# Output projection of an attention kernel: two batches in one 256-column matmul, in other places of TensorE's order

## The reference

```
# cross attention: q from layernorm(x), k and v from ctx, 16 heads of 8 features
score = einsum('bhij,bhkj->bhik', k, q) / sqrt(8)
attn  = softmax(score, axis=1)                 # over the heads
out   = einsum('bhik,bhij->bhjk', attn, v)
out   = out.transpose(0, 2, 1, 3).reshape(B, -1, 64).transpose(0, 2, 1)
x     = x + out @ Wo_w.T + Wo_b
# feed-forward on layernorm(x): three blocks of
#   y = gelu(layernorm(qlora_linear(h))); h = h + qlora_linear(y)
x     = x + ffn(layernorm(x))
```

## Time and profile before

| | us |
|---|---|
| median of 3 runs | 396.86 (396.68 to 397.3) |
| the profiled execution's own time | 397.27 |
| its span | 395.5 |
| TensorE busy (matmul) | 355.0 |
| VectorE busy | 345.6 |
| ScalarE busy | 289.6 |
| GpSimd busy | 283.1 |

### The profile page before, as it was taken

The page is one execution under the profiler, slowest core; times in us unless marked ns, Lnnn a source line. Parts: engine busy times, 40 slices in busy tenths (PEclk is TensorE's granted clock), DMA queues, the critical chain, the costliest instruction groups (busy, mean ns, idle before and its releaser), DMA issues.

```text
span 395.5 us, 12974 instructions
## 1 busy us (share of the span) xinstructions
PE 355.0 (90%) x4717; PEld 250.7 (63%) x4717; DVE 345.6 (87%) x863; ACT 289.6 (73%) x542; POOL 283.1 (72%) x349
## 2 busy tenths in 40 slices
PE   2788899999999999999897867789999999999964
PEld 1344566677766676677565645577778877887631
DVE  4618999999999999999999999688999999888852
ACT  3458888888878898788765443557888888888741
POOL 5463998888988898888998787757776667734320
PEclk9999999999999999999999989999999999999995
DMA  5755766558655775458424000000000100110111
GB/s 159 177 172 188 222 189 186 171 180 239 186 162 158 210 217 181 140 177 240 152 88 139 3 0 2 2 1 2 28 28 27 53 27 27 29 53 29 38 44 53
DMA packets 53123, 43.29 MB, mean 109 GB/s; under 512 B 4497, under 2 KB 46945, under 8 KB 53089
## 3 DMA queue, kind: packets, MB, share of 16 engines
q1 hardware_dynamic: 53088, 42.84, 36.0%
HBM read 26.05 MB, written 16.78 MB: 108 GB/s over the span
## 4 chain that ended last, share of the span: by engine, by line
PE 58%; DVE 20%; POOL 8%; issue 7%; ACT 4%; DMA 1%; DVEq 0%; POOLq 0%; ACTq 0%
PE score_ps L983 8%; DVE zsum L554 6%; PE att_ps L948 6%; DVE negmax L533 6%; PE score_ps L888 5%; PE wo_ps L840 5%; PE work L1030 4%; POOL probs L377 3%; PE score_ps L877 3%; PE work L904 3%; PE att_ps L1030 3%; PE score_ps L1030 3%; PE score_ps L976 2%; PE score_ps L834 2%; PE work L908 2%
## 5 line engine op out<-in xcount | busy, mean ns | idle before, releaser
L377 POOL TENSOR_TENSOR probs<-probs,rz 128x1024 f32<-128x1024 f32 x64 | 136.0, 2142 | 27.2 <-DVE rz L557 26.8
L413 POOL TENSOR_TENSOR rs<-ve,minus_half 128x8 f32<-128x8 f32 (+1 forms) x40 | 55.6, 1390 | 53.4 <-DVE ve L520 53.4
L533 DVE TENSOR_REDUCE negmax<-score_ps 128x64 bf16<-128x1024 f32 x64 | 75.3, 1177 | 6.9 <-PE score_ps L877 6.7
L663 ACT ACTIVATE probs<-score_ps 128x1024 f32<-128x1024 f32 x64 | 65.7, 1026 | 18.5 <-PE score_ps L888 18.2
L554 DVE TENSOR_REDUCE zsum<-probs 128x64 f32<-128x1024 f32 x64 | 77.3, 1209 | 1.3 <-ACT probs L663 1.3
L755 ACT ACTIVATE z<-score_ps,nmr,rs 128x128 f32<-128x128 f32 x160 | 60.4, 469 | 15.3 <-POOL nmr L416 15.2
L888 PE MATMUL score_ps<-negmax,ident_bf 128*128 128x512 bf16 x128 | 39.2, 388 | 8.3 <-DVE negmax L533 8.2
L840 PEld LDWEIGHTS wo_ps<-wo_t,att_t 128*128 128x128 f32 x256 | 37.5, 193 | 13.8 <-issue 12.2
L948 PE MATMUL att_ps<-probs,v_diag 128*32 128x64 f32 x2048 | 43.9, 225 | 2.1 <-POOL probs L377 1.9
L983 PEld LDWEIGHTS score_ps<-lin_t,h 128*128 128x128 f32 x320 | 42.1, 192 | 1.3
L983 PE MATMUL score_ps<-lin_t,h 128*128 128x128 f32 x320 | 42.2, 275 | 0.0
(11 more groups left out here) (152 smaller groups left out, 719.9 us busy)
## 6 DMA issues: line engine op xcount, KB each, us to landing
q_parts<-parts SPq DMA_DIRECT2D x16, 512.0 KB, 3.6
q_stack<-q_parts SPq DMA_DIRECT2D x64, 128.0 KB, 3.0
k_stack<-k_parts SPq DMA_DIRECT2D x32, 256.0 KB, 3.3
ctx_sb<-in_ctx SPq DMA_DIRECT2D x16, 256.0 KB, 3.7
k_parts<-parts SPq DMA_DIRECT2D x16, 256.0 KB, 3.0
out<-x_all SPq DMA_DIRECT2D x16, 256.0 KB, 2.3
x_all<-in_x SPq DMA_DIRECT2D x14, 256.0 KB, 3.9
x_all<-in_x SPq DMA_DIRECT2D x1, 512.0 KB, 4.9
```

Of the source, the lines that this page charges most:

```text
L377: nc.gpsimd.tensor_tensor(e[:, :, :, :], e[:, :, :, :], by_query.broadcast_to([P, BANDS, SEQ, ADJ]), ALU.mult).then_inc(s_probs, 1)
L413: nc.gpsimd.tensor_tensor(rs2[b][:, lo:hi], ve2[b][:, lo:hi], minus_half[:, lo:hi], ALU.pow).then_inc(p_rs[b], 1)
L533: nc.vector.tensor_reduce(negmax[p % 2][:, :], score_ps[p % 2][:, :].rearrange("p (h k) -> p k h", k=SEQ), AX_X, ALU.max, negate=True).the ...
L663: nc.scalar.activation(probs[p][:, :, :, :], score_ps[p % 2][:, :].rearrange("p (u s k) -> p u k s", s=ADJ, k=SEQ), ACT.Exp, scale=SCALE). ...
```

## The change

`project_out` takes a token tile u instead of a part t, and one matmul covers both batch halves, 256 columns, with the same weights. A chunk has 4 such matmuls instead of 8. The bias rows and tile 0 stand in position 1, behind the q matmul, and tile 1 in position 2, behind the k matmul, both for chunk c-2. Positions 0 and 3 have no output projection any more. The waits for att_t and for the sum of the chunk before move with the bias rows.

```diff
--- before.py
+++ after.py
@@ -833,12 +833,11 @@
                 src = src.unsqueeze(1).broadcast_to([P, TPC, P])
                 nc.tensor.matmul(dst, pick_row[:, which, :], src, start=True, stop=False, skip_group_check=True)
 
-            def project_out(t, att):
-
-                b, u = t % 2, t // 2
+            def project_out(u, att):
+
                 for o in range(2):
-                    ins = nc.tensor.matmul(wo_ps[:, TILE * t:TILE * (t + 1)], att[:, o, TILE * u:TILE * (u + 1)],
-                                           wo_t[:, o, b, :], start=False, stop=o == 1, skip_group_check=True)
+                    ins = nc.tensor.matmul(wo_ps[:, 2 * TILE * u:2 * TILE * (u + 1)], att[:, o, TILE * u:TILE * (u + 1)],
+                                           wo_t[:, o, :, :], start=False, stop=o == 1, skip_group_check=True)
                 return ins
 
             def chunk(c, par, half):
@@ -919,16 +918,14 @@
                                                    start=False, stop=True, skip_group_check=True)
                         ins.then_inc(s_v_ps, 1)
 
-                    if p == 3 and live(c - 1):
-                        pe.wait_ge(s_att_t, c)
-                        if some(c - 1):
-                            pe.wait_ge(s_x2, c - 1)
+                    if p == 1 and live(c - 2):
+                        pe.wait_ge(s_att_t, c - 1)
+                        if some(c - 2):
+                            pe.wait_ge(s_x2, c - 2)
                         bias_rows(wo_ps[:, :], 1)
-                        project_out(0, att_t[1 - par])
-                    if p < 3 and live(c - 2):
-                        ins = project_out(p + 1, att_t[par])
-                        if p == 2:
-                            ins.then_inc(s_wo, 1)
+                        project_out(0, att_t[par])
+                    if p == 2 and live(c - 2):
+                        project_out(1, att_t[par]).then_inc(s_wo, 1)
 
                     mc, mp = (c, p - 2) if p >= 2 else (c - 1, p + 2)
                     if live(mc):
```

## The result

| | before, us | changed, us | ratio |
|---|---|---|---|
| first comparison | 396.77 (4 runs) | 406.36 (404.81 to 406.79, 4 runs) | 1.0235 (1.0204 to 1.0265) |
| the changed kernel again | 397.24 (11 runs) | 404.27 (403.35 to 406.21, 6 runs) | 1.0186 (1.0152 to 1.022) |

A forecast was written before the change was run, and what follows sets the result against it. TensorE and VectorE were read as near full, with ScalarE's order limiting what TensorE could save. Cycles 7.6, less 0.4, plus 0.3 gave +7.5 us on 397.27: 404.8 profiled, median 404.4, range 400.0 to 406.0.

The forecast's parts named there:

- The pass: TensorE's output projection: a 256-column fp32 pass taken as 0.213 us, a block of four as 0.85, the 0.10 gap kept.
- rival C: Half the penalty: gap hidden, -0.2 a cycle, vanished x_all waits give back 2 us; +3.3, 400.2 us; chance 0.12.
- rival B: Width nearly free in TensorE's projection: 0.11 us a pass, cycle 12.52, 395.1 us, or no change; chance 0.05.
- T to Q: From position 3's scores (T) to position 1's query projection (Q): falls from 7.13 to 6.79 us, limited by ScalarE's order.
- Rival A: VectorE, not ScalarE's order, is the bound: cycle can fall to 12.44, 2.6 us off, 394.3 us; chance 0.07.
- Q to T: From the query projection to the next position 3 scores: 5.58 us grows by 1.03, less 0.03; nothing hides it.
- The cycle: One attention chunk, position 3's scores to the next: 13.37 us against 12.68, +0.69, over 11 cycles 7.6.
- Rival D: As forecast, plus 0.2 us a cycle from GpSimd's chain or lost overlap: +9.7, 406.6 us; chance 0.06.
- Chunks 13 to 17: Late chunks: -0.4 us of lateness given back, +0.3 for chunk 13's own cost, wider blocks hidden from chunk 14 on.
- at nothing, +-0.5: TensorE's three bias-row waits for the sum into x_all, 3.9 us, mostly vanish without VectorE profiting: nothing, +-0.5 us.
- The median: Whole kernel: profiled execution 404.8 us taken as 0.4 above the median, so median 404.4.
- Other engines: In the longer cycle VectorE's waits grow without effect, GpSimd's chain counts at nothing, no DMA moves.

The follow-up runs named there:

- width_spread: Changed kernel with its 256-column matmuls back in the old places, one in each position; 397.1 us, ratio to before 1.0014.
- after_filled: Changed kernel with extra bias matmuls in TensorE's two longest negmax waits, 8 in chunk 13 and 14 in chunk 15; 404.52 us, ratio to before 1.0218.
- after_half_xln: Changed kernel with two of the four normalisations of x left out from chunk 3 on; 401.68 us, ratio to before 1.0123.
- width_only: Changed kernel with bias rows and tile 0 moved to position 3, tile 1 to position 0, still 256 columns; 405.41 us, ratio to before 1.0203.
- tiles_p0_p2: Changed kernel with bias rows and tile 0 moved to position 0, tile 1 in position 2, 256 columns; 402.96 us, ratio to before 1.0166.

## Why the prediction was right or wrong

- *The pass.* Taken as 0.213, measured 0.215; four take 0.96 with the gap, so 0.85 and 0.10 stand. The gap isn't hidden, which takes rival C out, and the end of the bounds at 0.11 (rival B) is out. width_spread shows what the width makes alone: nothing. The Trainium skill (TensorE: Matmul & The Clock Gate, Back-to-back issue gap) gives 81 ns for a bf16 matmul of 128 columns and 131 ns for one of 512, from which the prediction read that width is nearly free. The fp32 rows don't show that: 0.215 for 256 columns is nearly twice the 0.11 for 128. Neither do the bf16 rows: the 14 extra matmuls of after_filled, of 512 columns and each with its weight load, follow each other at (3.19 - 0.38) / 13 = 0.216 us.
- *T to Q.* Forecast 6.79, measured 6.72. The 0.07 is the overlap ahead of xln_t: it starts 0.11 before the end of ctx_tr (164.96 against 164.48 + 0.59), where the forecast had 0.04. That ScalarE would be the limit there is shown by the cut of its work in both kernels. Rival A is out.
- *Q to T.* Forecast 5.58 + 1.03 - 0.03 = 6.58, measured 6.60.
- *The cycle.* Forecast 13.37, measured 13.32: +0.64 instead of +0.69, over 11 cycles 0.5 us less. Rival D's 406.6 is close to the median of the first comparison, but not its mechanism: it had 0.2 a cycle more, which no trace shows. The sum into x_all of chunk 12 trails T by 199.28 - 198.87 = 0.41, forecast 0.40. It comes 6.4 us later than before, where 7.6 - 0.4 = 7.2 were forecast; 0.3 of the difference is an earlier start of chunk 1 in this execution.
- *Chunks 13 to 17.* Here a step of the mechanism failed: "at nothing, +-0.5" and some 0.3 for chunk 13. From the sum of chunk 12 to the end of the span before took 202.57 us, the changed kernel 203.74 and, again, 204.23: 1.17 and 1.66 more. Chunk 13 gave 0.24 back instead of costing 0.3. Chunk 15 cost 1.35 in one trace, chunk 16 cost 1.83 in the other. In place of the term stands this: positions 0 and 3 have no projection any more, so where VectorE or GpSimd is the limit TensorE's waits run together (4.15 us where it was 3.08; 2.41 for GpSimd in chunk 16, where there had been 1.74 for the sum into x_all and a projection block), and half clock follows. In chunk 15 it falls on position 1 and 2 blocks that have become twice as long, ahead of scores that VectorE waits for; in chunk 16 it falls on the matmuls of the layer. In the six traces with half clock in chunk 15 whose blocks don't all stand in positions 1 and 2 there, the chunk takes 16.38 to 16.46 us; in the four where they do, 16.50 to 17.73. How much of the total is due to this isn't settled: single executions of the old order vary as well, and the four traces with the old places take 202.5 to 203.8 us for the same part.
- *The median.* This is the step that took the forecast out of its range. The prediction set the median 0.4 below the profiled execution, as it had been before, and so got 404.4 from 404.8. In the first comparison the profiled execution of before lay 0.5 above its median, and that of the changed kernel 1.55 below its own, the fastest of four: 7.5 + 0.5 + 1.55 = 9.6. In the second comparison the median is 404.27, inside the range. The two traces explain +7.5 and +8.3. The rest of the first comparison's +9.6 comes from executions of which there is no trace. Their mean granted clock, 0.968 to 0.976, points to more half clock than in the second comparison (0.972 to 0.981), but what it did and where was not shown, and this cause stays open. The range's upper end, 406.0, left no room for a term that varies by 3 us from execution to execution.
- *Other engines.* GpSimd as forecast: in the cycles of the changed kernel only TensorE's weight loads waited for it, three times, 0.5 us in all. It is near, as after_half_xln shows. DMA is in none of the waits of these cycles.

One thing wasn't seen ahead at all, though the sum didn't need it: the half from Q to T has a ScalarE floor as well. The expectation for width_only took 4.7 us for it and found 5.45.

## What to carry to other kernels

A block in an in-order queue is also a cover for the wait behind it, and its removal opens the wait. Before work is moved within a tight cycle, cut the cycle at the points where two engines meet and take for each part both the length on the moving engine and the floor that the other sets; a part gives back only down to its floor, and the other part pays in full. Halving the number of matmuls brings nothing where a pass costs its columns. And where waits are merged into longer ones late in the program, price the clock too. A median forecast from one profiled execution needs a range as wide as the spread of the executions, here 3 us.

## What the runs showed of the hardware

A 256-column fp32 pass costs 0.215 us, a 128-column one 0.11 and a 512-column one 0.425, with the weight load hidden in all three; a bf16 matmul of 512 columns costs 0.216. About 0.10 us are added where full-size matmuls are followed by the 32-column attention products. The mean granted clock of the executions of the kernel before on one chip ran from 0.969 to 0.994, with 398.3 to 393.8 us. In the late chunks half clock (1.2 GHz) mostly came during or just behind TensorE waits of 2.1 to 4.2 us. It did not come behind each: the wait of 2.50 in chunk 13 left the clock full in the changed kernel's first trace, a like one of 2.71 in tiles_p0_p2 did not. And it came without a long wait too: from 220.9 in the changed kernel's second trace, where the waits of the six us before are 0.95 and less.
